# An attention and quantised feed-forward layer on one core: loops written out, and three orders changed

## The reference

```python
q = x @ Wq.T + bq;  k_ = x @ Wk.T + bk;  v = x @ Wv.T + bv        # 16 heads of 32
bias = -inf for the 3 key columns with the largest band importance
attn = softmax(q k_^T / sqrt(32) + bias);  ctx = attn v
y = x + ctx @ Wo.T + bo
x1 = layernorm(x + layernorm(y) * gamma + beta)
xh = x1 @ H                        # 512 x 512 Hadamard matrix
xq = round(xh / s) * s, s = max|xh| / 7 of each token
out = layernorm(x1 + xq @ ternary(weight).T)
```

## Time and profile before

| | us |
|---|---|
| median of 3 runs (lowest, highest) | 4735.72 (4729.74, 4736.35) |
| the profiled execution, its own time | 4736.44 |
| its span | 4734.6 |

### The profile page before, as it was taken

One profiled execution on the slowest core, in us unless ns is written; L12 is line 12 of the kernel. 1 busy time (PEld: TensorE's weight loads), 2 busy tenths in 40 slices (PEclk: granted clock), 3 DMA queues, 4 the chain that ended last, 5 costly groups with the idle time before them and its releaser, 6 DMA issues.

```text
span 4734.6 us, 83913 instructions
## 1 busy us (share of the span) xinstructions
PE 4576.0 (97%) x24114; PEld 2400.6 (51%) x24152; DVE 3322.1 (70%) x5886; ACT 2527.3 (53%) x4891; POOL 3642.9 (77%) x1215
## 2 busy tenths in 40 slices
PE   7999999999899999999989999999999999999987
PEld 4445555554545555555454555555545555555434
DVE  4776777676677777666767767776776777777737
ACT  1555555554555555555455555555545555555545
POOL 1688888887488888888748888888865888888885
PEclk8999999999999999999999999999999999999988
DMA  7213333334422333332441223333334123332112
GB/s 172 72 41 72 64 69 72 66 70 108 104 64 46 65 73 69 77 71 59 116 115 42 57 62 72 72 66 70 77 110 103 42 55 70 73 68 61 30 55 73
DMA packets 245915, 346.30 MB, mean 73 GB/s; under 512 B 14801, under 2 KB 100561, under 8 KB 245458
## 3 DMA queue, kind: packets, MB, share of 16 engines
q1 hardware_dynamic: 243282, 339.68, 31.3%
q10 hardware_dynamic: 2176, 1.05, 0.2%
HBM read 205.33 MB, written 33.55 MB: 50 GB/s over the span
## 4 chain that ended last, share of the span: by engine, by line
PE 80%; POOL 12%; issue 4%; DVE 1%; ACT 1%; DMA 1%; SPq 0%; POOLq 0%; ACTq 0%; DVEq 0%
PE ps_s L552 21%; PE ps_m L537 20%; PE ps_o L582 18%; POOL acc L1146 7%; PE ps_z L557 6%; PE ps_z L524 5%; PE ps_z L492 4%; PE ps_m L498 3%; POOL prob L1172 1%; POOL prob L1176 1%; PE ps_s L498 1%; PE ps_s L492 1%; POOL prob L1161 1%; POOL prob L1155 1%; PE ps_m L667 1%
## 5 line engine op out<-in xcount | busy, mean ns | idle before, releaser
L957 DVE TENSOR_REDUCE umax<-ps_m 128x1 f32<-128x512 f32 x4096 | 2498.4, 680 | 705.3 <-PE ps_m L537 705.1
L1146 POOL TENSOR_TENSOR acc<-acc,prob 128x2048 f32<-128x2048 f32 x624 | 2858.5, 4581 | 134.6 <-ACT prob L801 85.0
L801 ACT ACTIVATE prob<-ps_s 128x512 f32<-128x512 f32 x4096 | 2063.7, 627 | 892.2 <-PE ps_s L552 875.7
L537 PE MATMUL ps_m<-kst,qst 97*128 97x512 f32 x4096 | 1714.7, 419 | 25.5 <-issue 16.5
L552 PE MATMUL ps_s<-qst,kst 99*128 99x512 f32 x4096 | 1656.1, 417 | 16.3 <-ACT prob L801 12.8
L537 PEld LDWEIGHTS ps_m<-kst,qst 97*128 97x128 f32 x4096 | 776.0, 190 | 543.9 <-DVE umax L957 310.2
L552 PEld LDWEIGHTS ps_s<-qst,kst 99*128 99x128 f32 x4096 | 774.8, 189 | 476.5 <-ACT prob L801 352.6
L582 PE MATMUL ps_o<-prob,vst 128*32 128x512 f32 x8192 | 976.2, 600 | 0.0
L1146 POOL TENSOR_TENSOR acc<-prob 128x2048 f32<-128x2048 f32 x64 | 290.9, 4545 | 343.3 <-ACT prob L801 343.3
L582 PEld LDWEIGHTS ps_o<-prob,vst 128*32 128x32 f32 x8192 | 227.7, 109 | 505.1 <-issue 293.1
L969 DVE RECIPROCAL zinv<-ps_z 128x512 f32<-128x512 f32 x64 | 214.9, 3358 | 265.5 <-PE ps_z L557 265.5
(11 more groups left out here) (120 smaller groups left out, 2530.7 us busy)
## 6 DMA issues: line engine op xcount, KB each, us to landing
xk<-in_xT_dram SPq DMA_DIRECT2D x66, 1024.0 KB, 8.6
xq<-in_xT_dram SPq DMA_DIRECT2D x65, 1024.0 KB, 5.8
kst<-hi SPq DMA_DIRECT2D x128, 256.0 KB, 6.8
qst<-hi SPq DMA_DIRECT2D x128, 256.0 KB, 5.6
wq<-in_wT_dram SPq DMA_DIRECT2D x65, 256.0 KB, 6.1
kst<-lo SPq DMA_DIRECT2D x64, 256.0 KB, 5.6
qst<-lo SPq DMA_DIRECT2D x64, 256.0 KB, 6.8
ctxT_dram<-obuf SPq DMA_DIRECT2D x64, 256.0 KB, 2.4
```

The costliest lines, as they stand in the source:

```text
L537: nc.tensor.matmul(ps_m[:, u % NMB, :], qst[k % 2][0:RSTACK, h, qt * P:(qt + 1) * P], kst[k // NQB % 2][0:RSTACK, h, kb * QB:(kb + 1) * QB ...
L801: nc.scalar.activation(prob[:, c % NPB, h, :], ps_s[:, (i * HG * NKC + HG * c + h) % NSB, :], ACT.Exp, scale=SCALE).then_inc(ex, 1)
L957: nc.vector.tensor_reduce(umax[:, m, kb:kb + 1], ps_m[:, u % NMB, :], AX.X, ALU.max).then_inc(mred, 1)
L1146: nc.gpsimd.tensor_tensor(acc[:], a, prob[:, c % NPB], ALU.add).then_inc(padd, 1)
```

## The change

1. `block_of`, `step_of` and the batch loop are gone: all four batches are written out, with constants as semaphore targets, on all five engines.
2. `qmask` moves to rows 16 to 19 of `prob`, partition 0. SP issues the eight mask copies behind the second key quarter instead of behind the fourth and the next stage's loads, and no longer waits for them before the queries.
3. The first maxima pass uses five PSUM banks, three of `ps_m` and two of `ps_s`.
4. In a token step DVE's chain of the norms comes first; the scaling of the feed-forward result moves behind the key projection's low part, directly ahead of the sum.

```diff
-def block_of(eng, b, i):
-    return eng.Fori(b * NBLK + i, b * NBLK + i + 1)
-def step_of(eng, b):
-    return eng.Fori(b, b + 1)
+        first_banks = [ps_m[:, 0, :], ps_m[:, 1, :], ps_m[:, 2, :], ps_s[:, 1, :], ps_s[:, 2, :]]
-        qmask = qst[0][0:1].rearrange("p h x -> p (h x)")
+        qmask = rows[0:1, 16:20, :].rearrange("p a n -> p (a n)")
...
-            keys(0, 0, 0)
-            next_stage(0, 0, 0)
-            sp.wait_ge(stk_ones, 4)
-            sp.wait_ge(mask_ok, 2)
-            for par in range(2):
-                for h in range(HG):
-                    sp.dma_start(kst[par][RMASK:RMASK + 1, h].bitcast(F32), qmask.bitcast(F32)).then_inc(mask_ld, 16)
-            sp.wait_ge(mask_ld, 2 * HG * 16)
+            for t in range(NQB):
+                keys_quarter(0, 0, 0, t)
+                if t == 1:
+                    sp.wait_ge(stk_ones, 4)
+                    sp.wait_ge(mask_ok, 2)
+                    for par in range(2):
+                        for h in range(HG):
+                            sp.dma_start(kst[par][RMASK:RMASK + 1, h].bitcast(F32), qmask).then_inc(mask_ld, 16)
+            next_block_x(0, 0, 0, 0)
+            next_block_x(0, 0, 0, 1)
+            next_weights(0)
             queries(0, 0)
             low_queries(0, 0)
...
-                elif u >= NMB:
-                    pe.wait_ge(mred, f * UNITS + u - NMB + 1)
+                elif u >= (len(first_banks) if first else NMB):
+                    pe.wait_ge(mred, f * UNITS + u - (len(first_banks) if first else NMB) + 1)
...
             def batch(b, last):
                 for i in range(NBLK):
-                    with block_of(pe, b, i) as n:
-                        attend(n, i, last)
+                    n = b * NBLK + i
+                    attend(n, i, last)
                 tokens(b, last)
-            with pe.Fori(0, NB - 1) as b:
+            for b in range(NB - 1):
                 batch(b, False)
             batch(NB - 1, True)
...
                 for s in range(STEPS):
-                    with step_of(dve, b) as bb:
+                    bb = b
...
                         q, f, y = s - 3, s - 4, s - 1
-                        if 0 <= f < NT:
-                            dve.wait_ge(c_ffn, bb * NT + (f + 1))
-                            nc.vector.scalar_tensor_tensor(out=ps_f[f % 2], in0=ps_f[f % 2], scalar=qsc[:, f % 2, 1:2],
-                                                           in1=wscale[:], op0=ALU.mult, op1=ALU.mult).then_inc(c_fs, 1)
                         norms = norms_of(s)
...
                        low_part(lo[:, k % 2], hi[:, k % 2], 1, NG + 1, ps_wo[(NT - 3) % 3]).then_inc(k_lo, 1)
+                    if 0 <= f < NT:
+                        dve.wait_ge(c_ffn, bb * NT + (f + 1))
+                        nc.vector.scalar_tensor_tensor(out=ps_f[f % 2], in0=ps_f[f % 2], scalar=qsc[:, f % 2, 1:2],
+                                                       in1=wscale[:], op0=ALU.mult, op1=ALU.mult).then_inc(c_fs, 1)
                     if 0 <= f < NT:
                         if f >= NST:
                             dve.wait_ge(c_st[f % NST], bb * (16 * stored_by(f % NST, NT)) + (16 + 16 * stored_by(f % NST, f)))
                         dve.wait_ge(c_fs, bb * NT + (f + 1))
                         nc.vector.tensor_tensor(tO[f % NST], ps_f[f % 2], tY[f % 4], ALU.add).then_inc(c_fo, 1)
```

More of the change, by code:

```diff
@@ new lines, in tokens @@
+                    if s == 2:
+                        wait_alone(pe, oz_cp, bb * NBLK + (NBLK + 1), passed)
+                        wait_alone(pe, zrec, bb * NBLK + (NBLK + 1), passed)
+                        wait_alone(pe, mcp, bb * NBLK + (NBLK + (0 if last else 1)), passed)
+                    t = s - 2
+                    if 0 <= t < NT:
+                        pe.wait_ge(c_w, bb * NT + (t + 1))
+                        if t >= 1:
+                            pe.wait_ge(c_wtc, bb * NT + t)
+                        for c in range(IC):
+                            mm = nc.tensor.transpose(ps_ht[:, c * P:(c + 1) * P], tH[t % 2][:, c * P:(c + 1) * P], ident[:])
+                        mm.then_inc(c_wt, 1)
@@ new lines, in tokens @@
+                    t = s - AGE[LN3]
+                    if 0 <= t < NT:
+                        act.wait_ge(c_rs, bb * (STEPS - 1) + s)
+                        nc.scalar.activation(tO[t % NST], tO[t % NST], ACT.Identity, scale=lnv[:, s % 2, LN3, 1:2],
+                                             bias=lnv[:, s % 2, LN3, 4:5]).then_inc(c_o, 1)
+                    t = s - KEY_STEP - 1
+                    if not last and 0 <= t < NQB:
+                        stage = bb * NG + (NG + 1)
+                        if t < 2:
+                            act.wait_ge(c_wo, bb * NT + NT)
+                        else:
+                            act.wait_ge(k_stk[t % 2], stage * (2 * NSTK) + NSTK)
+                        keys_of(stage, NG + 1, t, ps_wo[(NT - 3) % 3])
@@ new lines, in tokens @@
+                    t = s - 2
+                    if 0 <= t < NT:
+                        if t >= 2:
+                            act.wait_ge(c_h, bb * NT + (t - 1))
+                        act.wait_ge(c_wt, bb * NT + (t + 1))
+                        nc.scalar.activation(tHT[t % 2], ps_ht, ACT.Copy).then_inc(c_wtc, 1)
+                    t = s - KEY_STEP - 1
+                    if not last and 0 <= t < NQB:
+                        values_of(bb * NG + (NG + 1), NG + 1, t, ps_wo[(NT - 2) % 3])
@@ L889, in batch @@
                 for i in range(NBLK):
-                    with block_of(act, b, i) as n:
-                        attend(n, i, n >> 2, last)
+                    n = b * NBLK + i
+                    attend(n, i, n >> 2, last)
                 tokens(b, last)
-            with act.Fori(0, NB - 1) as b:
+            for b in range(NB - 1):
                 batch(b, False)
@@ new lines, in tokens @@
+                    if 0 <= q < NT:
+                        own()
+                        nc.vector.reciprocal(qsc[:, q % 2, 2:3], qsc[:, q % 2, 1:2]).then_inc(c_sc, 1)
+                    k = s - KEY_STEP - 1
+                    if not last and 0 <= k < NQB:
+                        stage = bb * NG + (NG + 1)
+                        dve.wait_ge(k_hi, stage * NQB + (k + 1))
+                        if k < 2:
+                            dve.wait_ge(c_xg, bb * NT + NT)
+                        else:
+                            dve.wait_ge(k_stk[k % 2], stage * (2 * NSTK) + NSTK)
+                        low_part(lo[:, k % 2], hi[:, k % 2], 1, NG + 1, ps_wo[(NT - 3) % 3]).then_inc(k_lo, 1)
@@ L1111, in batch @@
                 for i in range(NBLK):
-                    with block_of(dve, b, i) as n:
-                        if not (last and i == NBLK - 1):
-                            maxima(n + 1, i, last)
-                        inverse_sums(n)
+                    n = b * NBLK + i
+                    if not (last and i == NBLK - 1):
+                        maxima(n + 1, i, last)
+                    inverse_sums(n)
                 tokens(b, last)
-            with dve.Fori(0, NB - 1) as b:
+            for b in range(NB - 1):
                 batch(b, False)
```

448 lines of the change are left out of this document (201 added, 247 removed).

## The result

| kernel | median us (lowest, highest) | span of the profiled execution |
|---|---|---|
| before, beside it | 4734.43 (4729.74, 4736.35) | 4734.6 |
| changed | 4688.85 (4687.16, 4689.32) | 4687.4 |

The ratio is 0.9905, 95% interval 0.989 to 0.9919: 46 us less, where 49.6 were forecast. The mean granted clock was 0.986 against 0.983 before. Inside the blocks of batches 0 to 2 it is 1.00 in both, so it has no part in what the blocks gained; it differs at the start and between the batches, and is told there.

A forecast was written before the change was run, and what follows sets the result against it. PE was taken as the bound, 80% of the chain that ended last, with issue 4%. From 4736.4 us, 13.2 + 26.8 - 1.4 + 11.0 = 49.6 us less gave 4687 us; 8-in-10 range 4669 to 4706.

The forecast's parts named there:

- Back-edges and entry: Where the batch loop jumps back: without the jump, 6.6 us gained at each of two batch entries, 13.2 us.
- Blocks: Blocks of batches 0 to 2: constant semaphore targets save 0.80 us per projecting block, lose 0.16 in others; 26.8 us gained.
- Token steps: DVE's new order: steady step 7.55 us, 5.4 us lost in batches 0 to 2, 4 gained late in batch 3; 1.4 lost.
- The bound of 16 gained: Token steps, best case: 7.1 us a step if the square root hides, 16 us gained.
- the 5.4 us that I let the new order lose: Batches 0 to 2: 12 steady token steps each, 0.15 us longer than 7.40 under the new DVE order.
- The start: Before the first score: earlier first units from the mask move plus a shorter first maxima pass, 11.0 us gained.
- The mask move: Start: PE no longer waits for mask rows; units start 3.0 us earlier at best, 2.6 taken.
- The banks: First maxima pass: five banks save 1.2 us in each of seven groups, 8.4 us; bounds nothing and 10.
- A: Rival on DVE's order: L989 leaves the cycle, square root hides, steps 6.9 to 7.0 us; 4662 us; chance 0.08.
- B: Rival on constants: they don't carry over from batch 3, blocks give nothing; 4714 us; chance 0.09.
- C: Rival: slower than before, fetching the longer straight code stalls PE, 7.6 us each, 8 stalls net needed; chance 0.03.
- D: Rival: the start gives nothing, its pass being bound by loads or DVE; 4698 us; chance 0.08.

The follow-up runs named there:

- e7: The changed kernel with the one-trip loops around blocks and token steps put back, batch loop left out, semaphore targets still constants: 4687.6 us.
- e1: The kernel before with only batches, blocks and token steps written out; mask copies, banks and VectorE order as before: 4700.2 us.
- e3: The changed kernel with the feed-forward scaling back ahead of the chain in VectorE's token step: 4689.8 us.
- e2: The kernel before with the mask move, five banks and new VectorE order, but its batch loop and one-trip loops kept: 4717.0 us.
- e8: The changed kernel with another VectorE order, the subtraction that reads the mean ahead of the reciprocal and the residual sum moved later: 4685.6 us.
- e9: e8 with the mask copies at their old place and without SyncE's wait for them: 4687.6 us.

## Why the prediction was right, and where it was not

**Back-edges and entry** (13.2 us forecast). The issue pieces are gone, and the gaps between batches fell by 8.3 and 5.1 us, 13.4 together. Over the seven kernels from the changed one to e7 with constants the gap is 219.7 to 225.9 us, mean 222, against 228: 6 each, with a scatter of 3 us from how long the first token step takes (7 to 11 us). The jump shows without this scatter from the last chain of a token stage to the first reciprocal of the next batch: 64.4 and 64.3 us before, 57.6 and 57.7 now, and 57.6 at the end of the old batch 2, which has no jump. So 6.7 each: right. Part of it goes with the clock. The two windows from the end of batch 0 (before, then changed; PEclk is the third number from the end):

```profile
1288.40:1353.00 64.60, 57.00 (x285) 29.94 (x289) 42.04 (x76) 35.60 (x69) 45.82 (x10) 0.89 0.34 84
1272.50:1330.10 57.60, 54.95 (x285) 28.96 (x288) 41.64 (x75) 35.54 (x68) 45.83 (x10) 0.97 0.40 94
```

Without a jump the stretch takes 57.6 to 57.8 us where its granted clock is 0.97, and 58.7 to 59.5 where it is 0.94, in all kernels. The end of batch 2 in the changed kernel is one of the latter (59.1), which is where the time before batch 3 was lost.

**Blocks** (26.8). 8.7 + 8.9 + 8.9 = 26.5, with 62.41 us a projecting block in all batches and 3.86 us of idle where GpSimd is waited for. The old batch 3 was the right measure of the new batches 0 to 2, and e7 bears out that the loop heads cost nothing that can be measured. The blocks of batch 3 lost 1.7 us; its last four took 245.3 us in some executions and up to 248.7 in others, which I had not foreseen and no run explains.

**Token steps** (1.4 lost in the forecast, 4.5 gained in the traces). Size and mechanism of the step were right: 7.52 against 7.55, DVE idle 0.46 for the square root, and 3.7 us gained in the last token stage against 4. (The bound of 16 gained leaves out these 4; with them it is 20.) The step that was wrong here is the 5.4 us that I let the new order lose against 7.40: e1 has 7.52 with the old order, so the constants make the step longer, whatever the order. The whole token stages of batches 0 to 2 did not grow: 152.3, 154.8 and 152.8 us from first to last chain against 153.7, 153.3 and 153.4, since two later steps fell, from 8.7 to between 7.5 and 7.8 and from 10.0 to 9.4. And I saw only one of the two limits. That the wait for GpSimd's addition lay directly beneath was in the old trace, and I didn't read it. The timeline of DVE and POOL of the kernel before, in batch 3 and then in batch 0:

```profile
4645.37 1.29 POOL L1172 TENSOR_TENSOR prob<-lo,prob 128x512 f32<-128x512 f32 x1
4646.81 1.30 POOL L1176 TENSOR_TENSOR prob<-lo,prob 128x512 f32<-128x512 f32 x1
4647.90 0.23 DVE L1003 TENSOR_TENSOR lnv<-lnv 128x3 f32<-128x3 f32 x1
...
1201.81 1.29 POOL L1172 TENSOR_TENSOR prob<-lo,prob 128x512 f32<-128x512 f32 x1
1203.18 1.28 POOL L1176 TENSOR_TENSOR prob<-lo,prob 128x512 f32<-128x512 f32 x1
```

In batch 3 the chain's first two-input operation takes 0.23 us instead of 0.17 and ends at 4648.13, 0.02 us after the addition. In e1 and e3, the old order with constants, it takes 0.21 to 0.24 us in the steady steps of every batch, and ends 0.02 to 0.03 behind the addition, so there GpSimd holds the chain in every one of them.

**The start** (11.0). This is the part that failed: 5.8 us in this execution, and the two signs named for it did not come, with first units at 68.5 us for 64 and the first score at 133.1 for 128. In the eleven kernels with five banks the first reciprocal stands at 182.9 to 191.5 us, in the middle at 188.1, and in before and e1, whose start is the same, at 195.6 and 198.4, so some 8 or 9 on average.

The mask move, 2.6 forecast, came out as -2.0. The wait went, but the prediction let the copies push the loads by at most 1.5 us; the second wkv load was issued at 48.3 instead of 43.8 and took 14.0 us to land instead of 13.1. Where the loads did go out early, in e2 (45.2 us), the first units stand at 62.8, as the prediction's 63.5 would have it. The profiled execution of the kernel before was also a lucky one to reckon from: its wkv issue at 43.2 us is the earliest of all fourteen kernels.

The banks are the mis-sized term: 8.4 forecast, 4.8 measured. The pass itself gained 6.7, with PE stopped once in its second half, and the row of maxima then lost 2.4. The stop is not VectorE's pace, which the prediction named as a possible bound. The timeline of ACT, DVE and PE in the changed kernel:

```profile
106.64 0.69 ACT L752 ACTIVATE hi<-ps_z,bias 128x512 fp32r<-128x512 f32 x1 [11.90 <-DMA qst<-lo]
107.36 0.75 DVE L899 SCALAR_TENSOR_TENSOR lo<-ps_z,bias,hi 128x512 fp32r<-128x512 f32 x1 [4.17 <-ACT hi L752]
108.76 1.99 PE L529 MATMUL ps_m<-kst,qst 97*128 97x512 f32 x3 [3.94 <-DVE umax L950]
```

PE waits 3.94 us for VectorE, but VectorE has itself stood idle for 4.17, for ACT, and ACT for the DMA of the second query stack. This wait of PE is 2.3 to 4.1 us in all eleven kernels with five banks, and at most 0.8 in the three with three.

**The sum.** That 49.6 met 46 so closely is partly luck. By the trace the parts are 13.5 for the jumps, 26.5 for the blocks, 4.5 for the token stages and 5.8 for the start, less 1.3 before batch 3 and 1.7 in its blocks, which no term had. Blocks and jumps were met; the start gave 5.2 less than forecast and the token stages 5.9 more, and these two cancelled.

**Rivals.** A (7.0 us a step) did not happen, and e8 shows why its condition alone would not do: under the square root lay the held operation. B, C and D are excluded by the block spacings, by the absence of issue pieces inside batches, and by the first score at 133.1.

## What to carry to other kernels

Where one copy of a loop body in the old trace already runs with constants and without a jump, it is the measurement of what writing out the rest will bring; here it gave 26.8 us for 26.5. When taking away a wait changes nothing, look for an operation that has grown instead of for idle time: compare the duration of one small instruction with and without work on the neighbouring engine. And if two limits are equal, test them together, since each alone measures as nothing.

## What the runs showed of the hardware

A 128x3 VectorE operation with both inputs in SBUF took 0.73 to 0.81 us in the steady steps of e8 and e9 (and up to 1.2 us in single steps of the kernel before) instead of 0.17, ended 0.02 us behind GpSimd's addition, and counted as busy meanwhile; with one input in PSUM it took 0.16 us beside the same addition. An added 128x3 operation without a wait of its own cost 0.05 us a step, where one behind a semaphore takes 0.20. Semaphore targets in registers cost 0.8 us in a block of 63 us, but made the token step 0.12 us shorter (e1 against before): GpSimd's two additions followed each other at 1.37 us with registers and at 1.43 with constants, and with constants the chain is held behind the second. Why the additions stand further apart there stays open.
